# Pairs 11 to 20 of a graph-network kernel: the 512-deep matrix product in seven block products instead of eight

## What is computed

```
W = adj * adj                                   # elementwise, weighting
# layer 0, for each of the 64 matrices
h = max(layernorm(x), 0)
h = relu(W @ (h @ W1))      # W1 256 x 512
h = relu(W @ (h @ W2))      # W2 512 x 1024: the 512-deep product
x = x + W @ (h @ W3)        # W3 1024 x 256
# layer 1
U = eigenvectors of the normalised Laplacian of adj (256x256)
x = x + U @ (relu((U.T @ relu(layernorm(x))) @ V1 + c1) @ V2 + c2)
```

## Time and profile before

| | us |
|---|---|
| median of 3 runs | 2438.76 (2437.62 to 2440.72) |
| the profiled execution's own time | 2439.07 |
| its span, first to last instruction | 2437.3 |

### The profile page before, as it was taken

One profiled execution on the slowest core, in us unless ns is written; L12 is line 12 of the kernel. 1 busy time (PEld: TensorE's weight loads), 2 busy tenths in 40 slices (PEclk: granted clock), 3 DMA queues, 4 the chain that ended last, 5 costly groups with the idle time before them and its releaser, 6 DMA issues.

```text
span 2437.3 us, 43265 instructions
## 1 busy us (share of the span) xinstructions
PE 2395.8 (98%) x11564; PEld 1987.3 (82%) x11564; DVE 1887.6 (77%) x10013; ACT 877.5 (36%) x2386; POOL 369.5 (15%) x1196
## 2 busy tenths in 40 slices
PE   6999999999999999999999999999999999999999
PEld 4778877777788877778788778888888888889998
DVE  6888888888887676666666779599999994337776
ACT  3333333333333333333433333233232232225554
POOL 1111101111111111111111131000101000013332
PEclk9999999999999999999999999999999999999999
DMA  2000000000000000000000000000000001004443
GB/s 98 26 27 27 17 18 18 27 26 26 27 26 9 27 26 18 27 26 26 27 26 27 27 26 27 24 12 27 19 24 26 26 26 61 18 21 131 133 133 108
DMA packets 90002, 89.76 MB, mean 37 GB/s; under 512 B 5376, under 2 KB 89088, under 8 KB 89856
## 3 DMA queue, kind: packets, MB, share of 16 engines
q1 hardware_dynamic: 89856, 88.23, 11.3%
HBM read 54.66 MB, written 33.55 MB: 36 GB/s over the span
## 4 chain that ended last, share of the span: by engine, by line
PE 95%; DVE 3%; ACT 1%; issue 0%; SPq 0%; DMA 0%; POOL 0%; DVEq 0%; ACTq 0%; POOLq 0%
PE ps L1136 79%; PE ps L1313 9%; PE ps L1087 4%; PE ps L1323 1%; PE ps L1260 1%; DVE A L659 1%; DVE col L712 1%; DVE xc L717 0%; DVE prods L703 0%; DVE A L663 0%; SPq L270 0%; DMA xl<-in_x_dram 0%; DVE col L700 0%; DVE xrow_sb L668 0%; ACT squares L448 0%
## 5 line engine op out<-in xcount | busy, mean ns | idle before, releaser
L1136 PE MATMUL ps<-agg2T,w 128*128 128x256 f32 x4096 | 925.4, 380 | 0.5
L1136 PEld LDWEIGHTS ps<-agg2T,w 128*128 128x128 f32 x4096 | 757.7, 190 | 106.1 <-ACT agg2T L487 5.3
L1136 PE MATMUL ps<-w,hid2T 128*128 128x256 f32 x2048 | 462.9, 379 | 0.0
L1136 PEld LDWEIGHTS ps<-w,hid2T 128*128 128x128 f32 x2048 | 380.6, 190 | 51.2
L448 ACT ACTIVATE squares<-xrow_sb 128x128 f32<-128x128 f32 (+9 forms) x254 | 81.7, 322 | 791.8 <-DVE xrow_sb L668 791.7
L1136 PE MATMUL ps<-w,aggT 128*128 128x512 f32 x512 | 234.6, 596 | 0.5
L1136 PE MATMUL ps<-weightT,hid 128*128 128x256 f32 x1024 | 232.6, 379 | 0.0
L350 POOL COPY Eb<-sc 128x1 f32 (+1 forms) x254 | 47.1, 185 | 1151.1 <-DVE v L687 1151.1
L487 ACT ACTIVATE hid2T<-ps 128x512 f32<-128x512 f32 x256 | 149.3, 585 | 199.1 <-PE ps L1136 199.1
L1136 PEld LDWEIGHTS ps<-weightT,hid 128*128 128x128 f32 x1024 | 189.7, 190 | 32.9 <-issue 8.2
L792 DVE RECIPROCAL pinv<-ahead 128x40 f32<-128x40 f32 (+1 forms) x768 | 215.4, 322 | 0.1
(11 more groups left out here) (305 smaller groups left out, 3481.5 us busy)
## 6 DMA issues: line engine op xcount, KB each, us to landing
xl<-in_x_dram SPq DMA_DIRECT2D x64, 256.0 KB, 2.8
xr<-in_x_dram SPq DMA_DIRECT2D x64, 256.0 KB, 2.8
x_dram<-xr SPq DMA_DIRECT2D x64, 256.0 KB, 2.3
xin<-x_dram SPq DMA_DIRECT2D x64, 256.0 KB, 2.8
out_dram<-xin SPq DMA_DIRECT2D x64, 256.0 KB, 2.2
w<-in_L_gnn_W_dram SPq DMA_DIRECT2D x1, 2048.0 KB, 10.2
w<-in_L_gnn_W_dram SPq DMA_DIRECT2D x1, 1024.0 KB, 11.1
w<-in_L_gnn_W_dram SPq DMA_DIRECT2D x1, 512.0 KB, 3.7
```

The source lines that it names most:

```text
L1136: ins = pe.matmul(dst, a, b, start=start, stop=stop)
```

## The change

In pairs 11 to 20 the stage `hid2` is computed by Strassen's scheme. Its three matrices are seen as 2x2 blocks: W2 in 512 columns at a time (two halves, `half`), by 256 rows; `agg2T` by the two matrices of the pair (j) and 256 rows. Each half takes the seven block products P1 to P7, of four matmuls each, in place of eight: 56 products of a pair in place of 64. What is added for it:

- VectorE makes eight sums of blocks of W2 once (`sum_of_weights`, one behind each of the steps 24 to 31), in buffers that layer 1 uses later.
- In each pair VectorE makes four differences of blocks of `agg2T` (`sum_of_moving`) and fourteen additions of products, out of PSUM or SBUF (`add_products`), each on 128x512 fp32. They stand in one of two places of a step: inside `householder` between L697 and L700 of the listing above (called the first place here), or behind the whole step, so behind L663 (the second place). `beside7` gives at most two to a place.
- ScalarE copies four products (P1 and P7 of both halves) out of PSUM (`keep_product`), and applies Relu to the eight finished blocks in SBUF (`finish`), in place of eight evictions.
- TensorE waits for these sums, copies and additions at the head of each product (`product_waits`). The products of a pair are dealt out over its steps anew, 136 in place of 144.

The other pairs, the other stages and all transfers stay.

```diff
+        spare = ps[2:4]
...
+        def weight_sum(half, n):
+            return xin[:, 4 * half + n - 1, :, :]
...
+        def moving_sum(n):
+            return ahead[:, NB * N * (n - 1):NB * N * n].rearrange("p (b n) -> p b n", b=NB)
...
+        PRODUCTS = [("P1", 0), ("P1", 1), ("P2", 0), ("P2", 1)] + [(p, half) for half in range(2)
+                                                                  for p in ("P6", "P7", "P4", "P5", "P3")]
+        TO_KEEP = [("P1", 0), ("P1", 1), ("P7", 0), ("P7", 1)]
+        TO_ADD = [p for p in PRODUCTS if p not in TO_KEEP]
...
+        ADDS = [(("C11", half), ("P2", half)) for half in range(2)]
+        ADDS += [((name, half), (p, half)) for half in range(2)
+                 for name, p in (("U2", "P6"), ("U3", "P7"), ("C21", "P4"), ("U4", "P5"), ("C22", "P5"), ("C12", "P3"))]
+        ADD_AT = {name: n for n, (name, _) in enumerate(ADDS)}
...
+        WORK7 = [(i, m, size) for i, m, size in WORK if i < HID2_AT]
+        WORK7 += [(p, m, 1) for p in PRODUCTS for m in range(4)]
+        WORK7 += [(i, m, size) for i, m, size in WORK if i >= FIRST_G3]
...
+            moving = after_bucket(bucket(last[HID2_AT - 1]))
+            turns = {("T", n): moving + (n - 1) // 2 for n in range(1, 5)}
+            taken = {p: 2 for p in turns.values()}
+            p = moving + 2
+            for n, (_, product) in enumerate(ADDS):
+                p = max(p, after_bucket(bucket(last[product])))
+                while taken.get(p, 0) >= 2:
+                    p += 1
+                taken[p] = taken.get(p, 0) + 1
+                turns["add", n] = p
...
+            def keep_product(t, n, i):
+                act.wait_ge(prod, 4 * n + i + 1)
+                bank = (ring[2], ring[3], ring[1], ring[1])[i]
+                act.activation(kept_product(i), bank[:, :], ACT.Copy).then_inc(kept, 1)
+            def finish(t, n, i):
+                name, half = FINS[i]
+                act.wait_ge(added, len(ADDS) * n + ADD_AT[name, half] + 1)
+                act.activation(hid2_block(name, half), hid2_block(name, half), ACT.Relu).then_inc(evac, 1)
...
-            def householder(k, c0, bl):
+            def sum_of_weights(name, half):
+                n = int(name[1])
+                upper, lower = [w2_block(half, 0, k) for k in range(2)], [w2_block(half, 1, k) for k in range(2)]
+                a, b, op = {1: (lower[0], lower[1], ALU.add), 2: (weight_sum(half, 1), upper[0], ALU.subtract),
+                            3: (upper[0], lower[0], ALU.subtract), 4: (upper[1], weight_sum(half, 2), ALU.subtract)}[n]
+                if n in (2, 4):
+                    dve.wait_ge(sums_ready, 4 * half + n - 1)
+                dve.tensor_tensor(weight_sum(half, n), a, b, op).then_inc(sums_ready, 1)
+            def sum_of_moving(t, n):
+                q = t - SEVEN_FROM
+                a, b = {1: (agg2T[:, 1, 0:2, :], agg2T[:, 0, 0:2, :]), 2: (agg2T[:, 1, 2:4, :], moving_sum(1)),
+                        3: (agg2T[:, 1, 2:4, :], agg2T[:, 1, 0:2, :]), 4: (agg2T[:, 0, 2:4, :], moving_sum(2))}[n]
+                dve.wait_ge(evac, NU * t + (8, 9, 9, 9)[n - 1] + 3)
+                if n in (2, 4):
+                    dve.wait_ge(turn_s, 4 * q + n - 1)
+                dve.tensor_tensor(moving_sum(n), a, b, ALU.subtract).then_inc(turn_s, 1)
+            def add_products(t, n):
+                q = t - SEVEN_FROM
+                (name, half), product = ADDS[n]
+                bank = {"C11": spare[half], "U2": (ring[0], spare[1])[half], "U4": ring[2],
+                        "C21": (ring[3], ring[0])[half], "C12": (spare[0], ring[3])[half]}
+                p1, p7 = kept_product(half), kept_product(2 + half)
+                u3, u4 = hid2_block("C21", half), hid2_block("C12", half)
+                out, a, b = {"C11": (hid2_block("C11", half), p1, None), "U2": (p1, p1, None), "U4": (u4, p1, None),
+                             "U3": (u3, p1, p7), "C21": (u3, u3, None), "C22": (hid2_block("C22", half), u4, p7),
+                             "C12": (u4, u4, None)}[name]
+                if product in TO_ADD:
+                    dve.wait_ge(made, len(TO_ADD) * q + TO_ADD.index(product) + 1)
+                if name in ("C11", "U3"):
+                    dve.wait_ge(kept, 4 * q + (half if name == "C11" else 2 + half) + 1)
+                after = {"C11": None, "U2": "C11", "U4": "U2", "U3": "U2", "C21": "U3", "C22": "U4", "C12": "C22"}[name]
+                if after:
+                    dve.wait_ge(added, len(ADDS) * q + ADD_AT[after, half] + 1)
+                dve.tensor_tensor(out, a, bank[name][:, :] if b is None else b, ALU.add).then_inc(added, 1)
+            def householder(k, c0, bl, between=()):
...
+                for turn, arg, n in between:
+                    turn(arg, n)
                 done(11)
...
+                turns = beside7(steps, share)[2] if seven(first) else {}
                 for k in range(k0, k0 + steps * (last - first)):
-                    householder(k, columns(k0), blocks(k0))
+                    pair, which = divmod(k - k0, steps)
+                    here = [[(sum_of_moving if name == "T" else add_products, first + pair, n)
+                             for (name, n), p in turns.items() if p == 2 * which + place] for place in range(2)]
+                    householder(k, columns(k0), blocks(k0), here[0])
+                    for turn, arg, n in here[1]:
+                        turn(arg, n)
+                    if 0 <= k - S_FIRST < len(S_TURNS):
+                        if k == S_FIRST:
+                            dve.wait_ge(load_w, 16 * 7)
+                        sum_of_weights(*S_TURNS[k - S_FIRST])
...
+            def product_matmuls(p, half):
+                bank = {"P1": (ring[2], ring[3]), "P2": (spare[0], spare[1]), "P6": (ring[0], spare[1]),
+                        "P7": (ring[1], ring[1]), "P5": (ring[2], ring[2]), "P4": (ring[3], ring[0]),
+                        "P3": (spare[0], ring[3])}[p][half]
+                aggregated = [[agg2T[:, j, 2 * k:2 * k + 2, :] for k in range(2)] for j in range(2)]
+                left, right = {
+                    "P1": (w2_block(half, 0, 0), aggregated[0][0]), "P2": (w2_block(half, 0, 1), aggregated[0][1]),
+                    "P3": (weight_sum(half, 4), aggregated[1][1]), "P4": (w2_block(half, 1, 1), moving_sum(4)),
+                    "P5": (weight_sum(half, 1), moving_sum(1)), "P6": (weight_sum(half, 2), moving_sum(2)),
+                    "P7": (weight_sum(half, 3), moving_sum(3))}[p]
+                return sum([group(bank[:, N * c:N * c + N], [(left[:, d, P * c:P * c + P], right[:, d, :])
+                                                            for d in range(2)]) for c in range(2)], [])
...
+                elif p == "P7":
+                    turned_sum(3)
+                    evicted(9)
+                    if half:
+                        keeps(2)
+                elif p == "P5":
+                    turned_sum(1)
+                    keeps(0)
+                    if half:
+                        adds("U4", 0)
...
+            def product_work(t, n, p, half, m):
+                if m == 0:
+                    product_waits(t, n, p, half)
+                o, a, b, start, stop = product_matmuls(p, half)[m]
+                ins = pe.matmul(o, a, b, start=start, stop=stop)
+                if m == 0 and (p, half) == ("P3", 1):
+                    ins.then_inc(unit, len(FINS))
+                elif m == 3 and (p, half) in TO_KEEP:
+                    ins.then_inc(prod, 1)
+                elif m == 3:
+                    ins.then_inc(made, 1)
...
```

More of the change, by code:

```diff
@@ new lines, in gnn_spectral_kernel @@
+        S_TURNS = [(("S%d" % n), half) for half in range(2) for n in (1, 2, 3, 4)]
+        S_FIRST = 24
+        PRODUCTS = [("P1", 0), ("P1", 1), ("P2", 0), ("P2", 1)] + [(p, half) for half in range(2)
[3 more added lines that the diff above has]
+        ADDS = [(("C11", half), ("P2", half)) for half in range(2)]
@@ L494, in _ @@
             for (first, last, steps, share), k0 in zip(GROUPS, FIRST_STEP):
+                if seven(first):
+                    _, evictions, _ = beside7(steps, share)
+                    with act.Fori(first, last) as t:
+                        for s in range(steps):
+                            step_root(steps * t + (k0 - steps * first) + s, columns(k0))
+                            for e in evictions[s][0]:
+                                evict7(t, e)
+                            for j, at in enumerate(LN_AT):
+                                if 0 <= s - at < 6 and (s - at) % 2 == 0:
+                                    LN[(s - at) // 2](t + 1, j)
+                            for e in evictions[s][1] + evictions[s][2]:
+                                evict7(t, e)
+                        for e in evictions[steps][0]:
+                            evict7(t, e)
+                    continue
                 work_beside = beside(steps, share)
@@ new lines, in g3_work @@
```

(37 more changed lines are left out.)

100 lines of the change are left out of this document (97 added, 3 removed).

## The result

| | before | after |
|---|---|---|
| median, us | 2438.24 of 4 runs | 2468.01 of 4 (2467.84 to 2471.53) |
| profiled execution, us | 2439.07 | 2467.97 |
| its span, us | 2437.3 | 2466.2 |

The ratio is 1.0123, 95% interval [1.0111, 1.0136]: slower by 29.8 us where I had forecast 34, and inside the range.

The account below looks back on a forecast made before the run. TensorE bounds the kernel before; VectorE's loop would bound the change. Pairs sum 3 x 3.2 + 3 x 2.4 + 2 x 4.1 + 2 x 5.1 = 35.2, less 1.5: +34 us, 2472.5, range 2458 to 2490.

Parts of the forecast that it names:

- The loop of two engines: Pairs 11 to 20: additions lengthen VectorE's loop with TensorE beyond its slack, so VectorE's loop becomes the bound; chance 0.82.
- Steps 4 to 9 of pair 13: Steps with additions in both or one place: together 36.8 us against 32.4 before, +4.4; step 6 longest.
- The other steps: Pairs of twelve: step 2 has two products less, steps 10 and 11 one each, giving back 1.7 us.
- Step 3: Pairs of twelve: two additions in the second place lengthen the way from L700 to the copy, +0.7 us.
- the price of an addition: On VectorE's queue: 0.63 us for one, 1.36 for two in one place; less 0.25 in the second place.
- The same by groups of pairs: Loss per pair: 3.2 us in 11 to 13, 2.4 in 14 to 16, 4.1 in 17 and 18, 5.1 in 19 and 20.
- 1.5 for edges: Pairs 11 to 20: taken off because TensorE runs on into a late step's slack in a few steps.
- At nothing: Eight sums of weights behind steps 24 to 31, and ScalarE's copies and Relus: forecast to cost nothing.
- The rival that the additions hide: Pairs 11 to 20: TensorE stays the bound and 34.5 us are gained, 2404; decides at about 0.3 us an addition; chance 0.03.
- ScalarE as third party: Step 7 or 9 of a pair: copies and Relus delay the root, some 2 us a pair, 2493; chance 0.10.
- The clock: TensorE, idle in half a dozen steps a pair, falls to 1.2 GHz; 100 us more, 2573; chance 0.02.
- TensorE's idle time: Over pairs 11 to 20, expected at about 34 + 34.5 us in the profile after.

Follow-up runs that it names:

- Experiment 1: The change with every sum of pairs 11 to 20 narrowed to one column, waits, copies, Relus and products kept; 2409.06 us.
- 2: The kernel before with its eight products, plus 18 free-standing additions a pair at the change's places; 2477.94 us.
- 4: The kernel before with eight products, plus 18 free-standing additions a pair spread evenly over the steps, none behind a pair's last; 2444.92 us.
- experiment 8: The change with ScalarE's four copies and eight Relus of a pair narrowed to one column each; 2470.81 us.
- e4_gpsimd: The change with the four differences of the moving blocks of a pair made by GpSimd in place of VectorE; 2479.93 us.

## Why the prediction was right, and where it was off

- **The loop of two engines** was the mechanism. Experiment 1 shows that the additions' length is what costs, 2 that it costs without Strassen's products, 4 that it costs little where no step gets much more than it has to spare. Steps 4 to 9 of pair 13, forecast at 6.32, 5.59, 7.05, 6.32, 6.32 and 5.21 us, took 6.22, 5.41, 7.00, 6.00, 6.19 and 5.14.
- **The other steps**: the products taken out of steps 2, 10 and 11 were to give 1.7 us a pair; steps 0, 1, 2, 10 and 11 of pair 13 took 26.33 us for 28.03, 1.7 less. Step 3 was to lose 0.7 and lost 0.4.
- **The size was off by 4.4 us in the stage** (33.7 for 29.3). The term was the price of an addition. In the first place I took 0.63; a single one cost 0.60, so a wait for semaphores that is met held up nothing, where I had put a few hundredths. I took nearly all couples as dependent, at 1.36; that of step 7 was not and cost 1.19, the others 1.40. In the second place I took 0.63 - 0.25 = 0.38 and 1.11, by reckoning from the end of the second update; but the addition starts 0.24 us behind that update's start (965.28, 965.52), 0.08 ahead of its end, and cost 0.26 and 1.05. With these prices the six steps of pair 13 come to 36.15 for my 36.8; they took 35.96.
- **The same by groups of pairs**: I had forecast 9.6, 7.2, 8.2 and 10.2, less 1.5 for edges, and 7.6, 4.6, 7.7 and 9.3 came. The largest miss is in pairs 14 to 16 (2.32, 1.48 and 0.83 us): their steps 4 to 9 took 35.66, 35.20 and 35.19 us where I had 36.1, and the last step of pair 16 took 5.21 for 6.22. The total of 29.8 also holds what lies outside the stage, which the forecast put at nothing and which nearly cancels: 1.4 us less ahead of pair 11, 1.1 more behind step 253.
- **At nothing**: the eight sums of weights cost 0.08 us in all over steps 24 to 31. The Relus and copies cost nothing (experiment 8).
- **The rival that the additions hide** fell: an addition costs 0.60, twice the 0.3 at which it would have decided. **ScalarE as third party** fell with experiment 8: its Relus wait for the additions (32.4 us in the waits above), and VectorE's wait for its root is 49.3 us for 49.6 before. **The clock** stayed at 1.00, though TensorE stood idle up to 2.2 us in a step (step 7 of pair 17: 6.71 us from x transpose to x transpose, ten products).
- **TensorE's idle time** grew by 29.3 + 34.5 = 63.8 us counted by products; the busy table shows 48.2 us idle for 3.5, since a MATMUL row reaches beyond the start of the next.
- **What is not settled**: the 0.10 to 0.26 us in every fourth step of pairs 4 to 10 in two of the experiments, and whether the real additions can be spread enough to gain.

## What to carry to other kernels

Where two engines hand a column to and fro, count for each step what the loop of the idler engine has over, at the place where the work goes in; its busy share (70% here) says nothing. The same 180 additions cost 38 us where a step got up to four of them and 5 us spread out evenly, both beside eight products; beside seven, spread out, they cost 21. Keep neighbours on an engine independent (some 9 us here), and don't hand such work to GpSimd while VectorE reads SBUF in a tight loop.

## What the hardware showed beyond what I had expected

- A 128x512 fp32 addition of 0.68 to 0.69 us lets an operation that needs nothing of it start 0.60 us behind its own start; one that reads its result, and waits for semaphores as here, starts 0.78 to 0.79 behind, more than the 0.72 of the earlier trace rows.
- A GpSimd addition of 1.26 us holds a VectorE operation that starts during it and reads two tensors from SBUF until its end: 0.14 to 0.22 us became 1.08 to 1.31, 0.32 became 1.34. The copies out of PSUM that started beside one (15 in e4_gpsimd, at most 0.29 us) kept their length, and so did 128x1 operations that read one tensor (0.15 to 0.20).
- The granted clock stayed at 1.00 over pairs 11 to 20 though TensorE stood idle 0.4 to 1.8 us in each of the long steps (4 to 9 in pair 13, from x transpose to x transpose).
